# Convolution, attention and feed-forward in one kernel: two attention weights loaded five granules later, three raw weight chunks of each new sweep mixed ahead of it

## What is computed

```python
x = lax.conv_general_dilated(inputs, conv_w, (1,), 'SAME',
                             dimension_numbers=('NWC', 'WIO', 'NWC')) + conv_b   # conv_w: 3 taps, 1024 -> 768
q, k, v = jnp.split(x, 3, axis=-1)
# per block of 128: heads from q, k, v by wq, wk, wv; causal softmax; o by wo; then proj_w
x = layernorm(inputs + attention)
# base linear 1024 -> 1024, gate over 8 experts of rank 16, thresholds, mixture
x = layernorm(x + ffn)
```

## Time and profile before

| | |
|---|---|
| median of 3 runs | 1572.31 us (1571.24 to 1580.3) |
| the profiled execution's span | 1572.8 us |
| PE busy | 1541.9 us, 98% |
| DVE busy | 1181.8 us, 75% |
| ACT busy | 610.3 us, 39% |
| POOL busy | 256.3 us, 16% |
| mean granted TensorE clock | 0.995 of 2.4 GHz |

### The profile page before, as it was taken

The page is one execution under the profiler, slowest core; times in us unless marked ns, Lnnn a source line. Parts: engine busy times, 40 slices in busy tenths (PEclk is TensorE's granted clock), DMA queues, the critical chain, the costliest instruction groups (busy, mean ns, idle before and its releaser), DMA issues. The chain is left out here.

```text
span 1572.8 us, 29280 instructions
## 1 busy us (share of the span) xinstructions
PE 1541.9 (98%) x10816; PEld 1375.7 (87%) x10816; DVE 1181.8 (75%) x2792; ACT 610.3 (39%) x1732; POOL 256.3 (16%) x227
## 2 busy tenths in 40 slices
PE   7999999999999999999999999999999999999997
PEld 7999999999878888888888887898988999989987
DVE  8859967887876666666666677787788888788875
ACT  4224223322466767676676677211111111111110
POOL 0000000000000101010000113433333333333331
PEclk9999999999999999999999999999999999999999
DMA  8987774678810100101010222312211112211111
GB/s 323 370 308 272 257 256 166 240 279 282 280 68 1 55 20 34 53 0 53 0 53 0 76 93 77 108 61 74 76 61 60 60 60 75 75 60 60 60 55 44
DMA packets 55301, 181.05 MB, mean 115 GB/s; under 512 B 5568, under 2 KB 13888, under 8 KB 48704
## 3 DMA queue, kind: packets, MB, share of 16 engines
q1 hardware_dynamic: 53504, 173.81, 31.5%
q10 hardware_dynamic: 1728, 6.29, 1.0%
HBM read 125.49 MB, written 54.53 MB: 114 GB/s over the span
## 5 line engine op out<-in xcount | busy, mean ns | idle before, releaser
L976 ACT ACTIVATE scores_and_probs<-scores_and_probs,score_neg_max 128x128 f32<-128x128 f32 x512 | 198.0, 391 | 2.1 <-DVE score_neg_max L1077 2.1
L943 POOL TENSOR_TENSOR weights<-conv_tile,weights 128x1024 fp32r<-128x1024 f32 x14 | 35.7, 2552 | 860.7 <-ACT weights L962 775.7
L1072 DVE CUSTOM_DVE_ANT_0 scores_and_probs<-bankb,causal_mask 128x128 f32<-128x128 f32 x256 | 59.2, 288 | 114.6 <-PE bankc L1201 114.2
L1428 ACT ACTIVATE gate_exp<-h_and_gate,gate_neg_max 128x8 f32<-128x8 f32 x32 | 9.7, 302 | 347.9 <-DVE gate_neg_max L1503 347.9
L380 ACT ACTIVATE x_split<-x_planes 128x1024 fp32r<-128x1024 f32 x47 | 49.9, 1061 | 169.6 <-PE bankf L657 126.7
L1168 PE MATMUL bankg<-weights 128*128 128x512 f32 x378 | 103.2, 408 | 0.6 <-DVE v_heads L1062 0.5
L1187 PE MATMUL bankh<-weights 128*128 128x512 f32 x384 | 99.0, 393 | 1.7 <-DVE probs_T L1090 1.7
L1187 PE MATMUL banka<-weights 128*128 128x512 f32 x384 | 98.3, 391 | 0.8
L976 ACT ACTIVATION_READ_ACCUMULATOR scores_and_probs<-scores_and_probs,score_neg_max 128x1 f32 x512 | 97.5, 190 | 0.0
L511 DVE TENSOR_TENSOR x_split<-x_planes,x_split 128x1024 fp32r<-128x1024 f32 x47 | 57.4, 1222 | 49.8 <-ACT x_split L380 49.8
L657 PE MATMUL banka<-x_split,weights 128*128 128x256 f32 x576 | 77.8, 283 | 13.2 <-DVE weights L615 8.7
(11 more groups left out here) (244 smaller groups left out, 3885.0 us busy)
## 6 DMA issues: line engine op xcount, KB each, us to landing
x_raw<-in_xT SPq DMA_DIRECT2D x31, 1028.0 KB, 7.1
conv_tile<-in_x SPq DMA_DIRECT2D x32, 512.0 KB, 3.6
out<-out_tile SPq DMA_DIRECT2D x32, 512.0 KB, 2.7
conv_tile<-convT_scratch SPq DMA_DIRECT2D x16, 768.0 KB, 6.5
ce_scratch<-conv_l SPq DMA_DIRECT2D x16, 512.0 KB, 7.5
x_planes<-ce_scratch SPq DMA_DIRECT2D x16, 512.0 KB, 4.9
conv_y<-in_conv_w SPq DMA_DIRECT2D x6, 1152.0 KB, 6.5
convT_scratch<-conv_y SPq DMA_DIRECT2D x12, 512.0 KB, 6.1
```

What stands on the lines that cost most here:

```text
L943: nc.gpsimd.tensor_tensor(cs[:, LO, a:b, :], craw[:, a:b, :], cs[:, HI, a:b, :].bitcast(F32), ALU.subtract).then_inc(c_lo, 1)
L976: last = nc.scalar.activation(probs[:, s % 2, i, :], probs[:, s % 2, i, :], ACT.Exp, bias=ntop[:, s % 2, i:i + 1], scale=SCORE_SCALE, accu ...
L1072: last = nc.vector.tensor_tensor_reduce(out=probs[:, s % 2, i, :], in0=ps_s[h][:, n * P:(n + 1) * P], in1=mask[:], scale=1.0, scalar=LOWES ...
```

## The change

Two edits. `load_first_weights()` is called at j = 41 in place of j = 36. And at each turn of sweep, DVE mixes the new sweep's first three raw chunks in the three granules ahead of its first split, one in each; before it mixed the first chunk in the granule ahead and the two others between the splits of the first granule. The number and kind of instructions are the same.

```diff
@@ sync
-            if j == 36:
+            if j == 41:
                 load_first_weights()
@@ change_weights
             for s in range(1, SW):
                 g = j - (GRAN * NU * s - 1)
-                if g == -1:
-                    mix_weights(CC * s)
+                if -WR <= g < 0:
+                    mix_weights(CC * s + WR + g)
                 if 0 <= g < GRAN:
                     for c in range(CPG * g, CPG * g + CPG):
-                        if c + 1 < CC:
+                        if WR <= c + 1 < CC:
                             mix_weights(CC * s + c + 1)
                         split_weights(CC * s + c)
```

## The result

| | before | after |
|---|---|---|
| median of 4 runs | 1574.49 us (1571.24 to 1580.3) | 1562.97 us (1562.27 to 1563.98) |
| span of the profiled execution | 1572.8 us | 1560.5 us |
| PE busy | 1541.9 us | 1532.8 us |
| matmuls in a 40 us stretch of the convolution | 342 or 356 | 355 |

The ratio is 0.9925, with a 95% interval from 0.9902 to 0.9947: 0.75% faster, 11.5 us by the medians of these four executions each. Of the two numbers that the sum was made of, the stalls came true and the pace did not. Twelve more executions of the same kernel had a median of 1576.8, and twelve more again 1576.9. The rest is about what that means.

The account below looks back on a forecast made before the run. PE, busy 98% of the span, was taken as the bound, with its waits and matmul pace. From 1572.8: - 0.4 - 5.8 + 9.2 = 1575.8, or 1575.3 us on the runs' scale; range 1564 to 1579.

Parts of the forecast that it names:

- the stalls: PE's waits at both turns of sweep and the half-clock stretch behind them: 0.4 and 5.8 us expected to go.
- the chain behind granule 36: PE's 3.3 us late start there, traced through ACT's evacuation and late planes to the 2 MB weights and a full DVE.
- DVE's split of granule 19 at 169.8: At the first turn of sweep, this split ends 2.3 us earlier; PE needs it at 171.87, a margin of 2.1 us.
- The pace as a quantity of its own: PE's convolution matmuls run at 117.9 or 113.5 ns at one granted clock, turning only at a pause of PE.
- I take the pace to be slow from 19 us on, as in the trace: Assumed 117.9 ns matmuls up to 172 us, as profiled before, with nothing turning the pace before the next pause.
- the term of +9.2 us: Convolution from granule 19: without the pause, 2088 matmuls stay slow at 4.4 ns each; chance of slow to the end 0.45.
- fast from 19 us on: Rival: the start at 19.12 draws the fast pace, 5.7 us more gained than fast from granule 19; 1560.4, chance 0.05.
- The slow case itself: Slow pace to the convolution's end: last matmul at about 418 us, span 1575.8, time 1575.3; chance 0.45.
- The collision at granule 41: Rival: the moved 2 MB delay planes 41 past 346 us, making PE late at granule 40; 1580.3, chance 0.06.
- its price of nothing: Moved 2 MB make DVE wait 1 to 2 us for a reload; costed at nothing, PE's x being two granules ahead.
- The page's rule of one gap: Skill's N/2.4 + 2.5 ns, 109.2 ns for 256 columns, cited for the rival of fast pace anyway: 1566.1, chance 0.27.

## Why the prediction was right or wrong

*What bounds the kernel, and the chain behind granule 36:* right. The stalls went with the change, 5.8 us at the second turn and 0.4 at the first; the repeat of the kernel before had the same chain with a longer stall.

*First turn of sweep, DVE's split of granule 19 at 169.8:* right for the pace that it was worked out for. The second profile of the changed kernel, slow from 44 us on, has it at 169.4 and PE at 171.5, a margin of 2.1 us; the first, fast throughout, has 165.65 and 166.54. The pause went in both, but at the fast pace with only 0.9 us to spare.

*The pace as a quantity of its own, kept between pauses and changed only at one:* right, in every profile. It never changed but at a late start of PE, though 0.07 us late was enough once.

*"I take the pace to be slow from 19 us on, as in the trace":* this step failed, and with it the term of +9.2 us for the slow pace to the end. In the first profile of the changed kernel that term measured 0, and the 18 granules ahead of 172 us, which I had left slow, gave back another 5.7 us. The median of the four runs is that of the rival "fast from 19 us on", to which I gave a chance of 0.05. I read one execution's draw as the program's. The error has two parts. The kernel before has no fixed pace either: in the second profile of it the stretch that had been slow was fast. And the pause at 44 us, at unit 1's start, which the profile before did not show at all (PE, being slow, came there too late to wait), draws again. Of the 18 profiles of all kernels here, 13 have it; the pace ahead of it was fast in all 13, and behind it slow in nine. It is the last pause of the changed kernel, so what it leaves stays to the end. Over 28 executions the changed kernel is at 1577.2 in 18 and at 1563.4 in 10; a forecast of two groups, with the share open, would have been the right form.

*The sizes, once the pace is known:* near. The single figure 1575.3 is 1.9 us below the upper group, and the rival's 1560.4 is 3.0 below the lower. Of these, 2.3 us are in the scale: I set the profile's span 0.5 us above the time of the runs, while for every execution with both the time is 1.8 us above the span (1562.27 and 1560.5). The slow case itself, a last matmul at about 418 and a span of 1575.8, is what the second profile has: 417.3 and 1575.2.

*The collision at granule 41:* the transfer was delayed as feared, 6.2 us of waiting on DVE, and PE had the cover for it. The wait was forecast too short, and for the wrong transfer; its price of nothing was right.

*The page's rule of one gap:* the Trainium skill (TensorE: Matmul & The Clock Gate, "Back-to-back issue gap") gives 109.2 ns by its formula for 256 columns, which it calls the gap of isolated matmuls; of streams with a weight load before each matmul, as here, it says that both set the spacing, and has figures for 128 and 512 columns only. The runs show 113.3 and 117.8 ns at a granted clock of 1.00 for one instruction stream, which differ by 14 us over the convolution. Against the formula's single gap, the measurement decides.

*What the change is worth.* At the fast pace about 10 us, by an estimate: the second profile of the kernel before spans 1574.6 us with 12 x 72 slow matmuls, which at the fast pace would be 3.8 us less, 1570.8; the changed kernel, fast throughout, spans 1560.5. No profile here shows the kernel before slow throughout, so the worth at the slow pace stays open; the repeated profile of the changed kernel, slow from 44 us on, spans 1575.2, no less than the kernel before in either of its profiles. Over many executions the mean went from 1575.1 (131 executions, 1568.9 to 1581.1) to 1572.3, 0.18% or 2.8 us with some 1.3 us of uncertainty. But without the first four it is 1573.8, and each repeat by itself can't be told from no change: the ratios are 0.9979 (0.9953 to 1.0005) and 0.9997 (0.9974 to 1.0021). The load alone, which keeps the pauses, is shown faster, at 0.9979 (0.9968 to 0.9990). The 0.75% of the first comparison is one of the two outcomes of the changed kernel.

*Still open:* what the hidden part of a restart is, what sets its first value, why the pause at 44 us turned the pace to slow in nine of 13 profiles, and why the first four executions of the changed kernel were all in the lower group; at a share of 6 in the 24 others that is a chance of 1 in 256, and the chip of those four isn't known to be one of the others.

## What to carry to other kernels

Before costing a removed stall, count the matmuls per microsecond on both sides of each pause: if the rate differs at the same granted clock, as it did here, the kernel has a second state that the pause selects, and one profile shows one draw of it. Ask too whether the waits that you remove had been taking back what the higher rate gains; without them it shows in full, and so does the lower one. Take several executions of each kernel and look at the list of times, not at the median; two groups with nothing between are a finding in themselves. And a load that collides with a stage's turn can go to where the engines' inputs are granules ahead, even if it delays just as much there.

## What the runs showed of the hardware that I had not expected

Float32r matmuls of 256 columns, each with its own weight load, run at 113.3 or 117.8 ns apart, with the granted clock at 1.00 in both. The pace is kept over thousands of matmuls (3384 in the longest stretch, from 19.4 us to the end of the convolution in the profile with two banks in turn) and changes only where PE starts late, 0.07 us being enough in one case and 0.1 us in several. Evenly spaced short pauses that PE makes by waiting for its own last matmul act alike within an execution: alternating, always fast, or always slow; close pairs can change from one to the other. Neither the order of the PSUM banks nor the number of matmuls between the pauses has a part in it.
